# Self-attention's output product: seven tiles for four heads, with the first head's second tile moved by small transfers into idle rows of the other three's

## The chip, the cores and the metric

One core of one Trainium2 chip runs the whole kernel in one launch. The metric is the device time in microseconds, the median of several runs. TensorE multiplies matrices, ScalarE, VectorE and GpSimd (POOL in the rows) work on elements, and SyncE (SP in the rows) does nothing here but issue DMA transfers, one after another in the order in which they stand in its program.

## What is computed

A decoder layer over 32 sequences of 256 tokens with 256 features: self-attention, cross-attention against a context of 120 rows, and a mixture of 16 experts, each followed by a residual sum and a layer norm. The change lies in self-attention alone, 16 heads that share one latent of 72 columns:

```python
Wdkv = x @ latent_w + latent_b                                    # (b, t, 72), keys and values alike
q = einsum('btc,hcl->bhtl', x, Wd_w) + Wd_b                       # 16 heads of 72
scores = einsum('bhtl,bsl->bhts', q, Wdkv) / sqrt(16), causal
y = einsum('bhts,bsl->bhtl', softmax(scores), Wdkv)               # (b, h, t, 72)
z = transpose(y, (0, 2, 1, 3)).reshape(b, t, 16 * 72)
x = layernorm(x + z @ out_w + out_b)                              # the output product
```

## The kernel before

All products are of float32 values split in two: a high part, rounded to the format that TensorE takes at its fast rate, and a low part, what the rounding left. A product a x w is a_hi w_hi + a_lo w_hi + a_hi w_lo. For the general case that is three matmuls (`three`, L128 to L132). Where the contraction is over 72 rows only, a tile of TensorE's 128 rows has room for more than one of the three, and two matmuls do (`two`, L135 to L139):

- The first tile has y_hi[0:72] in rows 0 to 71 and y_hi[16:72] once more in rows 72 to 127, against w_hi[0:72] and w_lo[16:72].
- The second tile has y_lo[0:72] in rows 0 to 71 and y_hi[0:16] in rows 96 to 111, against w_hi[0:72] and w_lo[0:16]. Rows 72 to 95 are idle, against weights of zero. Rows above 111 are not read.

REST = 16 and AT = 96 are the names of these places, L = 72 is a head's rows. The repeated rows of y_hi come for free, since the latent has its columns repeated. The 16 rows in the second tile are a copy by GpSimd (L575), and y_lo is what VectorE subtracts (L909).

**The stage.** Two sequences are a group, and 16 groups make the stage. A group has 16 slots, u = 0 to 15, and slot g of the stage is for one pair of heads p = g % 16 // 2 and one sequence i = g % 2 of its group c. Each engine runs through the slots in the same order, with a lag for each step, so that in slot m there stand beside one another: scores of g = m - 6 (SL), normalising of m - 7 (IL), transposes of the probabilities of m - 8 (TL), the product with the values and y_hi, y_lo of m - 10 (PL), and the output product of m - 12 (OL). Buffers for y, q, and the probabilities are rings of 4 (RING). In 9 of the 16 slots (Q_SLOT: 2, 3, 5, 6, 8, 9, 11, 12, 14) a tile of q for both sequences is made: six matmuls, ScalarE's high part (L790), VectorE's low part (L898).

**The q moves.** A tile of q is 128 rows, and heads of 72 rows don't align with it. So SyncE moves the rows of each head from q_tile to their place in q by transfers within on-chip memory: the rows (L503), those that stand there twice (L506) and the 16 of the second tile (L510), 5 to 8 transfers a tile, 63 in a group. They have 8 to 72 partitions. The moves of tile t stand in SyncE's program in the slot of tile t, behind a wait for its low part (qlo_done). The scores of pair p (slot 2p + 6) wait on TensorE for tiles p and p + 1 (q_in), and ScalarE's high part of tile t waits for the moves of tile t - 2.

SyncE also loads xT for the next group in slot 3 (L412), the residual rows in slots 13 and 14 (L523), and stores x1 in slots 2 and 5 (L526). From slot 40 of the stage on it carries a staging of the cross-attention's weights, 16 pieces at 6 slots from one another: a load (L486) and, 6 slots later, two stores (L491).

The program's order on each engine is written out by hand in the `slot` functions of `sync`, `gpsimd`, `tensor`, `scalar` and `vector`; nothing reorders it. The body of 32 slots is a loop, with the first and last bodies written out.

The output product of a slot before, 8 matmuls of 256 columns:

```python
for hh in range(2):
    w = slice((2 * p + hh) * C, (2 * p + hh + 1) * C)
    for t in range(TT):
        mm = two(pe, O[i][:, t * C:t * C + C], y_hi[:, r, hh, tk], y_lo[:, r, hh, tk], ow[:, 0, w], ow[:, 1, w], ...)
```

Of the kernel before, what the change touches and what calls it, by code (L numbers as in the profile page):

```python
# [177 lines left out]
SA_BODY = 32  # L178
SA_BODIES = B * NP // SA_BODY
# [90 lines left out]
def self_attention(nc, al, bank, ident, cross, d):  # L270
# [13 lines left out]
    minus_low = al.sb("minus_low", [P, 1])  # L284
# [58 lines left out]
    ydup_done = al.sem("ydup_done")  # L343
    q_mm, qhi_done, qlo_done = al.sem("q_mm"), al.sem("qhi_done"), al.sem("qlo_done")
# [32 lines left out]
    sthi_done, stlo_done = Later(owhi_done, NP), Later(ow_done, NP)  # L377
# [28 lines left out]
    def sync(sp):  # L406
# [67 lines left out]
        def slot(J, m):  # L474
# [55 lines left out]
    def gpsimd(pool):  # L530
# [11 lines left out]
                           pattern=[[0, 1]], channel_multiplier=1).then_inc(const, 1)  # L542
# [13 lines left out]
        def slot(J, m):  # L556
# [14 lines left out]
            if slot_exists(J, g):  # L571
# [3 lines left out]
                pool.tensor_scalar(y_lo[AT:AT + REST, r], f32(y_hi[0:REST, r]), 1.0, 1.0, ALU.mult, ALU.mult).then_inc(ydup_done, 1)  # L575
# [33 lines left out]
    def tensor(pe):  # L609
# [33 lines left out]
        def slot(J, m):  # L643
# [77 lines left out]
            if slot_exists(J, g):  # L721
# [3 lines left out]
                if first_body(J) and c == 0 and i == 0:  # L725
                    pe.wait_ge(ow_done, p + 1)
# [13 lines left out]
    def scalar(act):  # L740
# [30 lines left out]
        def slot(J, m):  # L771
# [21 lines left out]
            if slot_exists(J, g):  # L793
# [4 lines left out]
                need(act, o_mm, upto_slot(J, g - RING))  # L798
                act.activation(y_hi[:, r].rearrange("l h t -> l (h t)"), PV[:], ACT.Copy).then_inc(yhi_done, 1)  # L799
# [1553 lines left out]
```

## Time and profile before

| | |
|---|---|
| median of 3 runs | 3112.0 us (3110.74 to 3114.18) |
| the profiled execution, its own time | 3109.2 us |
| its span, first to last instruction | 3107.3 us |
| mean granted TensorE clock | 0.998 |
| TensorE busy, share of the span | 99% |
| TensorE weight loads | 93% |
| VectorE / ScalarE / GpSimd | 73% / 69% / 51% |
| self-attention on TensorE | 0 to 1175 us |
| output product, first tiles | 1024 matmuls, 278.1 us busy, 303 ns each |
| output product, second tiles | 1024 matmuls, 257.6 us busy, 282 ns each |

The time is that of the run, the span that of the instructions in it. Busy times of matmuls overlap, as one starts while the one before it still runs: what a matmul costs is the distance between two starts. In the rows, PE is TensorE, PEld its weight loads, DVE VectorE, ACT ScalarE, POOL GpSimd, and SPq SyncE's queue, whose entries show how long an issue occupied it and not how long the transfer took. `<-` before a name gives who ended an idle time.

### The profile page before, as it was taken

How to read it: one execution, taken by the hardware profiler on the slowest of the kernel's cores; microseconds unless marked ns; L12 is line 12 of the kernel's file. 1: busy time of each engine (PE TensorE's matmuls, PEld its weight loads, DVE VectorE, ACT ScalarE, POOL GpSimd, SP SyncE). 2: the span in 40 equal slices, each digit the busy share in tenths (PEclk: the TensorE clock that was granted, in tenths of full speed). 3: DMA queues.
4: the chain of work that ended last, by engine and by line, in shares of the span. 5: the costliest groups of instructions: out<-in, count | busy, mean ns of one | idle time of the engine just before them, and what ended most of it. 6: DMA issues, size and time to landing. Idle time of an engine off the chain costs nothing. (4 is left out here: it accounts for less than half of the span.)

```text
span 3107.3 us, 72903 instructions
## 1 busy us (share of the span) xinstructions
PE 3080.1 (99%) x22657; PEld 2894.1 (93%) x22657; DVE 2259.1 (73%) x6587; ACT 2146.8 (69%) x6949; POOL 1591.9 (51%) x2918
## 2 busy tenths in 40 slices
PE   9999999999999999999999999999999999999998
PEld 7999999999999998999999999999988888889998
DVE  7888888887777877778878777887865555444665
ACT  8888888888888887787887877887744444442222
POOL 5677677666676665333333333333456666652000
PEclk9999999999999999999999999999999999999999
DMA  5455555444444460211111211211255445433333
GB/s 166 125 148 159 150 151 153 138 121 125 123 113 114 126 212 30 65 45 49 62 45 49 62 49 45 63 48 48 102 133 113 101 102 115 115 54 89 125 125 101
DMA packets 202273, 315.29 MB, mean 101 GB/s; under 512 B 34752, under 2 KB 135744, under 8 KB 200928
## 3 DMA queue, kind: packets, MB, share of 16 engines
q1 hardware_dynamic: 177376, 277.82, 29.6%
q0 software_dynamic: 24576, 33.57, 6.3%
q8 instruction: 155, 2.54, 0.4%
q14 instruction: 166, 1.36, 0.1%
HBM read 125.20 MB, written 75.50 MB: 65 GB/s over the span
## 5 line engine op out<-in xcount | busy, mean ns | idle before, releaser
L1131 POOL TENSOR_SCALAR ca_prob<-ca_prob,ca_inverse 128x120 f32<-128x120 f32 x1024 | 354.7, 365 | 618.9 <-DVE ca_inverse L1433 616.9
L820 ACT ACTIVATE sa_prob<-sa_prob,sa_shift 128x128 f32<-128x128 f32 (+1 forms) x1024 | 453.7, 462 | 0.0
L1373 ACT ACTIVATE ca_prob<-bank,ca_shift 128x120 f32<-128x120 f32 x1024 | 354.9, 368 | 3.5 <-DVE ca_shift L1427 2.2
L875 DVE CUSTOM_DVE_ANT_0 sa_prob<-bank,sa_mask 128x128 f32<-128x128 f32 (+1 forms) x1024 | 304.3, 351 | 0.9 <-issue 0.2
L566 POOL TENSOR_SCALAR sa_prob<-sa_prob,sa_inverse 128x128 f32<-128x128 f32 x512 | 199.4, 389 | 199.0 <-DVE sa_inverse L887 190.2
L137 PE MATMUL bank<-sa_ow,sa_y_hi 128*128 128x256 f32 x1024 | 278.1, 303 | 0.0
L139 PE MATMUL bank<-sa_kvT_b,sa_q 112*128 112x128 f32 (+1 forms) x1024 | 260.6, 280 | 0.0
L916 DVE TENSOR_TENSOR sa_pT_lo<-bank,sa_pT_hi 128x384 fp32r<-128x384 f32 x512 | 257.9, 543 | 0.2 <-ACT sa_pT_hi L807 0.2
L139 PE MATMUL bank<-sa_ow,sa_y_lo 112*128 112x256 f32 x1024 | 257.6, 282 | 0.0
L137 PE MATMUL bank<-sa_kvT_a,sa_q 128*128 128x128 f32 (+1 forms) x1024 | 248.9, 279 | 1.0 <-DVE sa_shift L875 0.7
L568 POOL TENSOR_SCALAR sa_prob<-sa_prob,sa_inverse 128x256 f32<-128x256 f32 x512 | 245.2, 479 | 0.0
L1866 POOL DMA_INDIRECT mid_acc<-ex_out,ex_to_tokens x112 | 191.1, 1706 | 87.4 <-DVE ex_out L2178 59.6
L909 DVE TENSOR_TENSOR sa_y_lo<-bank,sa_y_hi 96x512 fp32r<-96x512 f32 x256 | 174.9, 683 | 73.7 <-ACT sa_y_hi L799 73.2
L2056 ACT ACTIVATE ex_act_g<-bank 128x512 f32<-128x512 f32 x128 | 76.5, 598 | 215.2 <-PE bank L132 207.3
L807 ACT ACTIVATE sa_pT_hi<-bank 128x384 fp32r<-128x384 f32 x512 | 222.8, 493 | 0.5 <-PE bank L710 0.3
L1373 ACT ACTIVATION_READ_ACCUMULATOR ca_prob<-bank,ca_shift 128x1 f32 x1024 | 219.9, 215 | 0.0
L799 ACT ACTIVATE sa_y_hi<-bank 128x512 fp32r<-128x512 f32 x256 | 153.1, 598 | 95.6 <-PE bank L132 95.0
L820 ACT ACTIVATION_READ_ACCUMULATOR sa_prob<-sa_prob,sa_shift 128x1 f32 x1024 | 211.1, 206 | 0.0
L710 PE MATMUL bank<-all_ident,sa_prob 128*128 128x128 f32 x1536 | 209.8, 272 | 1.3 <-POOL sa_prob L568 1.3
L1333 ACT ACTIVATE ca_q_hi<-bank 128x256 fp32r<-128x256 f32 x256 | 99.0, 387 | 159.6 <-PE bank L132 153.4
L2143 DVE TENSOR_TENSOR ex_hid<-ex_act_g,bank 128x512 f32<-128x512 f32 x128 | 87.9, 687 | 162.2 <-PE bank L132 154.6
L137 PEld LDWEIGHTS bank<-sa_kvT_a,sa_q 128*128 128x128 f32 x1024 | 195.3, 191 | 2.1 <-DVE sa_shift L875 1.2
(274 smaller groups left out, 12039.2 us busy)
## 6 DMA issues: line engine op xcount, KB each, us to landing
sa_q<-sa_q_tile SPq DMA_DIRECT2D x125, 288.0 KB
sa_q<-sa_q_tile SPq DMA_DIRECT2D x157, 112.0 KB
mid_x2T<-ca_x2T SPq DMA_DIRECT2D x32, 512.0 KB, 3.0
ex_sx<-mid_x2T SPq DMA_DIRECT2D x32, 512.0 KB, 3.4
sa_q<-sa_q_tile SPq DMA_DIRECT2D x297, 32.0 KB
sa_xT_raw<-in_xT SPq DMA_DIRECT2D x32, 256.0 KB, 2.9
sa_q<-sa_q_tile SPq DMA_DIRECT2D x32, 256.0 KB
sa_x_res<-in_x SPq DMA_DIRECT2D x32, 256.0 KB, 3.0
```

The source lines that it names most:

```text
L137: pe.matmul(out, stat_hi, mov_hi, start=start, stop=False, skip_group_check=True)
L139: return pe.matmul(out, stat_lo[rows], mov_lo[rows], start=False, stop=stop, skip_group_check=True)
L566: pool.tensor_scalar(prob[:, r, hh, 0:P], prob[:, r, hh, 0:P], inverse[:, r, 2 * hh:2 * hh + 1], 1.0, ALU.mult, ALU.mult)
L568: pool.tensor_scalar(prob[:, r, hh, P:3 * P], prob[:, r, hh, P:3 * P], inverse[:, r, 2 * hh + 1:2 * hh + 2], 1.0, ALU.mult, ALU.mult).then ...
L710: mm = pe.transpose(TR[hh][:, n * P:n * P + P], prob[:, r, hh, n * P:n * P + P], ident[:])
L807: act.activation(pT_hi[:, r, hh], TR[hh][:, 0:3 * P], ACT.Copy).then_inc(pThi_done, 1)
L820: act.activation(prob[:, r, hh, cols], prob[:, r, hh, cols], ACT.Exp, bias=shift[:, r, n:n + 1], scale=-1.0, accum_out=total[:, r, n:n + 1 ...
L875: dve.tensor_tensor_reduce(out=prob[:, r, hh, cols], in0=SC[hh][:, t * T:t * T + (t + 1) * P], in1=mask[:].rearrange("p a s -> p (a s)")[: ...
L916: dve.tensor_tensor(pT_lo[:, r, hh], TR[hh][:, 0:3 * P], f32(pT_hi[:, r, hh]), ALU.subtract).then_inc(pTlo_done, 1)
L1131: ins = pool.tensor_scalar(prob[:, r, t, hh], prob[:, r, t, hh], inverse[:, r, n:n + 1], 1.0, ALU.mult, ALU.mult)
L1373: act.activation(prob[:, r, t, hh], SC[g % 2][:, n * S:n * S + S], ACT.Exp, bias=shift[:, r, n:n + 1], accum_out=total[:, r, n:n + 1]).the ...
L1866: pool.indirect_dma_start(d["acc"].rearrange("b t c -> (b t) c"), bass.IndirectOffsetOnAxis(ap=of[:, j:j + 1], axis=0), out[:, i, t], None ...
```

## The change

For a quad of four heads, two pairs, the first head loses its second tile. What stood in it is put into idle rows of the second tiles of the other three: y_lo[0:24] into rows 72 to 95 of head 1's, y_lo[24:48] into those of head 2's, y_lo[48:72] into those of head 3's, and y_hi[0:16] into rows 112 to 127 of head 2's. The weights' second tile (`ow_b`) is laid out on the host to match. Since partitions change, the rows go by DMA, four transfers on SyncE's queue in every slot of an even pair:

- the near one (L504 of the changed kernel), 24 partitions x 1 KB, in the slot in which y_lo is made, ahead of the q moves, behind a wait for ylo_done. It goes to the same pair's other head, and the output product of that pair waits for it (y_near) two slots later;
- the far ones (L529 to L531), 24, 16 and 24 partitions x 1 KB, after the q moves of that slot, behind a wait for the output product of two slots before in the ring (o_mm). They go to the next pair, whose output product waits for them (y_far) four slots later. ScalarE waits for them too, before it overwrites y_hi.

GpSimd's copy leaves out the first head, VectorE's y_lo has 72 partitions in place of 96, and the split of the output weights is two instructions in place of one, with a scalar of its own for each tile. In the output product all first tiles now come ahead of the second tiles.

```diff
+QUAD = 4
+GAP = AT - L
...
-    minus_low = al.sb("minus_low", [P, 1])
+    minus_low = al.sb("minus_low", [P, 2])
...
+            g = m - PL
+            if slot_exists(J, g) and g % QUAD < 2:
+                r, i = g % RING, g % 2
+                need_alone(sp, ylo_done, upto_slot(J, g), spare_sp)
+                sp.dma_start(f32(y_lo[L:AT, r, 1]), f32(y_lo[0:GAP, r, 0])).then_inc(y_near[i], 16)
             c, u = m // GROUP, m % GROUP
             t = tile_at(J, m)
...
+            g = m - PL
+            if slot_exists(J, g) and g % QUAD < 2:
+                r, i = g % RING, g % 2
+                n = (g + 2) % RING
+                need(sp, o_mm, upto_slot(J, g - 2))
+                sp.dma_start(f32(y_lo[L:AT, n, 0]), f32(y_lo[GAP:2 * GAP, r, 0])).then_inc(y_far[i], 16)
+                sp.dma_start(f32(y_lo[P - REST:P, n, 0]), f32(y_hi[0:REST, r, 0])).then_inc(y_far[i], 16)
+                sp.dma_start(f32(y_lo[L:AT, n, 1]), f32(y_lo[2 * GAP:L, r, 0])).then_inc(y_far[i], 16)
...
-                pool.tensor_scalar(y_lo[AT:AT + REST, r], f32(y_hi[0:REST, r]), 1.0, 1.0, ALU.mult, ALU.mult).then_inc(ydup_done, 1)
+                own = slice(int(g % QUAD < 2), 2)
+                pool.tensor_scalar(y_lo[AT:AT + REST, r, own], f32(y_hi[0:REST, r, own]), 1.0, 1.0, ALU.mult, ALU.mult).then_inc(ydup_done, 1)
...
-                for hh in range(2):
+                ahead = (y_near if p % 2 == 0 else y_far)[i]
+                for a, hh in ((0, 0), (0, 1), (1, 1)) if p % 2 == 0 else ((0, 0), (0, 1), (1, 0), (1, 1)):
                     w = slice((2 * p + hh) * C, (2 * p + hh + 1) * C)
+                    if a == 1 and hh == 1 - p % 2:
+                        need(pe, ahead, upto_quad(J, g, 16 if p % 2 == 0 else 48))
+                    rows = slice(0, AT + REST if a == 1 and (p % 2 == 0 or hh == 1) else P)
                     for t in range(TT):
                         tk = slice(t * P, t * P + P)
-
-                        mm = two(pe, O[i][:, t * C:t * C + C], y_hi[:, r, hh, tk], y_lo[:, r, hh, tk], ow[:, 0, w],
-                                 ow[:, 1, w], p == 0 and hh == 0 and t == 0, p == NP - 1 and hh == 1)
+                        mm = pe.matmul(O[i][:, t * C:t * C + C], (y_lo if a else y_hi)[rows, r, hh, tk], ow[rows, a, w],
...
+                if g % QUAD < 2:
+                    need(act, y_far[g % 2], upto_quad(J, g - QUAD, 48))
                 act.activation(y_hi[:, r].rearrange("l h t -> l (h t)"), PV[:], ACT.Copy).then_inc(yhi_done, 1)
...
-                dve.tensor_tensor(y_lo[0:AT, r].rearrange("l h t -> l (h t)"), PV[0:AT, :],
-                                  f32(y_hi[0:AT, r].rearrange("l h t -> l (h t)")), ALU.subtract).then_inc(ylo_done, 1)
+                dve.tensor_tensor(y_lo[0:L, r].rearrange("l h t -> l (h t)"), PV[0:L, :],
+                                  f32(y_hi[0:L, r].rearrange("l h t -> l (h t)")), ALU.subtract).then_inc(ylo_done, 1)
```

**SyncE, slots 2 and 3 of a group, before.** From the last moves of tile 0 (slot 2) to tile 1's last and the first load of xT. The shape is partitions x float32 elements of each.

```order
L506 DMA sa_q<-sa_q_tile 40x512
L510 DMA sa_q<-sa_q_tile 16x512
L526 DMA mid_x<-sa_x 128x2x256 [waits sa_x1_done]
L503 DMA sa_q<-sa_q_tile 16x1024 [waits sa_qlo_done,sa_s_mm]
L506 DMA sa_q<-sa_q_tile 16x512
L503 DMA sa_q<-sa_q_tile 72x1024
L506 DMA sa_q<-sa_q_tile 56x512
L510 DMA sa_q<-sa_q_tile 16x512
L503 DMA sa_q<-sa_q_tile 40x1024
L506 DMA sa_q<-sa_q_tile 24x512
L510 DMA sa_q<-sa_q_tile 16x512
L412 DMA sa_xT_raw<-in_xT 128x2x256 [waits sa_xlo_done]
```

**SyncE, the same place, changed** (the moves are now L516, L519 and L523, the store L547). From the same last moves of tile 0.

```order
L519 DMA sa_q<-sa_q_tile 40x512
L523 DMA sa_q<-sa_q_tile 16x512
L529 DMA sa_y_lo<-sa_y_lo 24x256 [waits early_sa_o_mm]
L530 DMA sa_y_lo<-sa_y_hi 16x256
L531 DMA sa_y_lo<-sa_y_lo 24x256
L547 DMA mid_x<-sa_x 128x2x256 [waits sa_x1_done]
L504 DMA sa_y_lo<-sa_y_lo 24x256 [waits sa_ylo_done]
L516 DMA sa_q<-sa_q_tile 16x1024 [waits sa_qlo_done,sa_s_mm]
L519 DMA sa_q<-sa_q_tile 16x512
L516 DMA sa_q<-sa_q_tile 72x1024
L519 DMA sa_q<-sa_q_tile 56x512
L523 DMA sa_q<-sa_q_tile 16x512
```

Three far transfers stand between tile 0's moves and the store, and a near one ahead of tile 1's moves. Tile 0's moves have a near one ahead of them in the same way, and three far ones follow tile 1's moves.

**TensorE, the output product of a slot and the scores of the next, before.**

```order
L137 MATMUL bank<-sa_ow,sa_y_hi 128x256 [waits sa_ydup_done,sa_ylo_done]
L139 MATMUL bank<-sa_ow,sa_y_lo 128x256
L137 MATMUL bank<-sa_ow,sa_y_hi 128x256
L139 MATMUL bank<-sa_ow,sa_y_lo 128x256
L137 MATMUL bank<-sa_ow,sa_y_hi 128x256
L139 MATMUL bank<-sa_ow,sa_y_lo 128x256
L137 MATMUL bank<-sa_ow,sa_y_hi 128x256
L139 MATMUL bank<-sa_ow,sa_y_lo 128x256
```

**TensorE, the same in a slot of an even pair, changed.**

```order
L759 MATMUL bank<-sa_ow,sa_y_hi 128x256 [waits sa_ydup_done,sa_ylo_done]
L759 MATMUL bank<-sa_ow,sa_y_hi 128x256 x3
L759 MATMUL bank<-sa_ow,sa_y_lo 128x256 [waits sa_y_near1]
L759 MATMUL bank<-sa_ow,sa_y_lo 128x256
L137 MATMUL bank<-sa_kvT_a,sa_q 128x128 [waits sa_s_read,sa_q_in1,sa_q_in0]
```

Six matmuls in place of eight, and a wait for the near transfer ahead of the last two. In a slot of an odd pair there are eight still, with a wait for the far ones ahead of the last four.

## Rows read from the trace of the kernel before

**Rows 1.** Windows: us, busy of each engine (instructions), PEclk, DMA share, GB/s.

```profile
100.00:200.00 100.00, 100.00 (x710) 93.22 (x709) 79.71 (x298) 82.03 (x268) 67.98 (x129) 1.00 0.50 135
700.00:800.00 100.00, 100.00 (x714) 93.29 (x713) 79.66 (x302) 80.89 (x263) 69.50 (x131) 1.00 0.41 115
...
1100.00:1200.00 100.00, 95.51 (x695) 89.80 (x694) 73.78 (x254) 72.93 (x253) 65.06 (x130) 0.98 0.46 154
```

**Rows 2.** Waits from 50 to 1170 us: total us, times, longest.

```profile
PEld bank L130 <- DVE sa_kv_lo L920: 2.3, 14, 0.2
...
PE bank L130 <- DVE sa_y_lo L909: 1.1, 2, 0.5
```

**Rows 3.** TensorE's timeline: starts of slots 0, 2, 6, 16, and two output matmuls.

```profile
706.38 0.22 PE L137 MATMUL bank<-sa_kvT_a,sa_q 128*128 128x128 f32 x1
...
715.40 0.22 PE L137 MATMUL bank<-sa_kvT_a,sa_q 128*128 128x128 f32 x1
...
719.88 0.28 PE L137 MATMUL bank<-sa_ow,sa_y_hi 128*128 128x256 f32 x1
...
720.36 0.28 PE L137 MATMUL bank<-sa_ow,sa_y_hi 128*128 128x256 f32 x1
...
734.17 0.22 PE L137 MATMUL bank<-sa_kvT_a,sa_q 128*128 128x128 f32 x1
...
778.46 0.22 PE L137 MATMUL bank<-sa_kvT_a,sa_q 128*128 128x128 f32 x1
```

**Rows 4.** The tile sa_q, SyncE, 706.4 to 778.4 us: ns min/median/max.

```profile
L503 SPq DMA_DIRECT2D sa_q<-sa_q_tile x24: 527/740/895, 719.7 to 775.6; - x24
L506 SPq DMA_DIRECT2D sa_q<-sa_q_tile x22: 583/748/807, 720.5 to 776.4; - x22
L510 SPq DMA_DIRECT2D sa_q<-sa_q_tile x17: 554/555/1788, 721.4 to 777.2; - x17
```

**Rows 5.** SyncE's timeline: partitions 128; 72; 16; 24; 16; 128; 24; 8.

```profile
705.76 0.58 SPq L523 DMA_DIRECT2D sa_x_res<-in_x  x1
719.70 0.79 SPq L503 DMA_DIRECT2D sa_q<-sa_q_tile  x1
...
724.99 0.55 SPq L503 DMA_DIRECT2D sa_q<-sa_q_tile  x1
...
729.29 0.72 SPq L506 DMA_DIRECT2D sa_q<-sa_q_tile  x1
730.05 0.56 SPq L510 DMA_DIRECT2D sa_q<-sa_q_tile  x1
730.65 1.09 SPq L412 DMA_DIRECT2D sa_xT_raw<-in_xT  x2
...
736.87 0.74 SPq L503 DMA_DIRECT2D sa_q<-sa_q_tile  x1
737.65 0.64 SPq L506 DMA_DIRECT2D sa_q<-sa_q_tile  x1
```

**Rows 6.** VectorE's timeline: y_lo of slot 2.

```profile
719.82 0.69 DVE L909 TENSOR_TENSOR sa_y_lo<-bank,sa_y_hi 96x512 fp32r<-96x512 f32 x1 [0.21 <-ACT sa_y_hi L799]
```

**Rows 7.** Timeline of the first group: a tile's last move, and who waited for it.

```profile
48.62 0.59 SPq L510 DMA_DIRECT2D sa_q<-sa_q_tile  x1
...
52.12 0.69 ACT L790 ACTIVATE sa_q_tile<-bank,sa_qbias 128x512 fp32r<-128x512 f32 x1 [2.24 <-DMA sa_q<-sa_q_tile]
```

**Rows 8.** DMA issues: KB each, median us from issue to landing.

```profile
mid_x<-sa_x SPq DMA_DIRECT2D x32, 256.0 KB, 2.3
```

**Rows 9.** SyncE's timeline: two pieces of the staging.

```profile
180.94 0.58 SPq L486 DMA_DIRECT2D early_st_raw<-in_wv  x1
...
182.05 0.85 SPq L491 DMA_DIRECT2D mid_cw<-early_st_lo  x1
...
452.40 0.39 SPq L486 DMA_DIRECT2D early_st_raw<-in_wq  x1
...
453.32 0.42 SPq L491 DMA_DIRECT2D mid_cw<-early_st_lo  x1
```

More of the change, by code:

```diff
@@ L202, in upto_tile, with upto_quad @@
     return J * (SA_GROUPS * QT * per) + (per * (t + 1) + more)
+def upto_quad(J, g, per=1):
+    return J * (SA_BODY // QUAD * per) + per * (g // QUAD + 1)
 def slot_exists(J, g):
@@ L343, in self_attention @@
     ydup_done = al.sem("ydup_done")
+    y_near, y_far = [al.sem(f"y_near{i}") for i in range(2)], [al.sem(f"y_far{i}") for i in range(2)]
     q_mm, qhi_done, qlo_done = al.sem("q_mm"), al.sem("qhi_done"), al.sem("qlo_done")
@@ L725, in slot @@
                 if first_body(J) and c == 0 and i == 0:
-                    pe.wait_ge(ow_done, p + 1)
+                    pe.wait_ge(ow_done, 2 * (p + 1))
                 if p == 0:
                     need(pe, o_read, upto_row(J, c, i - 2))
-                for hh in range(2):
+                ahead = (y_near if p % 2 == 0 else y_far)[i]
+                for a, hh in ((0, 0), (0, 1), (1, 1)) if p % 2 == 0 else ((0, 0), (0, 1), (1, 0), (1, 1)):
                     w = slice((2 * p + hh) * C, (2 * p + hh + 1) * C)
+                    if a == 1 and hh == 1 - p % 2:
+                        need(pe, ahead, upto_quad(J, g, 16 if p % 2 == 0 else 48))
+                    rows = slice(0, AT + REST if a == 1 and (p % 2 == 0 or hh == 1) else P)
                     for t in range(TT):
                         tk = slice(t * P, t * P + P)
-                        mm = two(pe, O[i][:, t * C:t * C + C], y_hi[:, r, hh, tk], y_lo[:, r, hh, tk], ow[:, 0, w],
-                                 ow[:, 1, w], p == 0 and hh == 0 and t == 0, p == NP - 1 and hh == 1)
+                        mm = pe.matmul(O[i][:, t * C:t * C + C], (y_lo if a else y_hi)[rows, r, hh, tk], ow[rows, a, w],
+                                       start=p == 0 and a == 0 and hh == 0 and t == 0, stop=p == NP - 1 and a == 1 and hh == 1,
+                                       skip_group_check=True)
                 mm.then_inc(o_mm, 1)
@@ L848, in split_ow @@
             dve.wait_ge(owhi_done, p + 1)
-            dve.scalar_tensor_tensor(out=part, in0=f32(part), scalar=minus_low[:, 0:1], in1=raw,
-                                     op0=ALU.mult, op1=ALU.add).then_inc(ow_done, 1)
+            for a in range(2):
+                cols = slice(C if a == 1 and p % 2 == 0 else 0, 2 * C)
+                dve.scalar_tensor_tensor(out=part[:, a, cols], in0=f32(part[:, a, cols]), scalar=minus_low[:, a:a + 1], in1=raw[:, a, cols],
+                                         op0=ALU.mult, op1=ALU.add).then_inc(ow_done, 1)
         def split_first_x(i):
@@ L2324, with filled @@
     ow = a("L0_attn_out_w").reshape(H, L, C).transpose(1, 0, 2).reshape(L, H * C)
+    def filled(h):
+        own, lent, n = ow[:, h * C:(h + 1) * C], ow[:, (h - h % QUAD) * C:(h - h % QUAD + 1) * C], h % QUAD
+        rows = np.zeros((P, C), ow.dtype)
+        if n > 0:
+            rows[:L], rows[L:AT], rows[AT:AT + REST] = own, lent[(n - 1) * GAP:n * GAP], own[:REST]
+        if n == 2:
+            rows[AT + REST:] = lent[:REST]
+        return rows
     laid = {
@@ L2331 @@
         "ow_a": again(ow, 0),
-        "ow_b": np.concatenate((ow, np.zeros((AT - L, H * C), ow.dtype), ow[:REST], np.zeros((P - AT - REST, H * C), ow.dtype))),
+        "ow_b": np.concatenate([filled(h) for h in range(H)], 1),
         "qbias": a("L0_attn_Wd_b").reshape(QT, P).T, "lbias": again(a("L0_attn_latent_b").reshape(L, 1), 0),
```

6 lines of the change are left out of this document (3 added, 3 removed).

## The prediction

> **What bounds the kernel now.** I read the windows by stage first, because the change lies in self-attention alone, the first 1175 us or so. In a window of that stage TensorE is busy for all of it, its weight loads for 93%, and VectorE, ScalarE and GpSimd for 70 to 81%, at the full granted clock [rows 1]. Next the list of waits of the stage: the longest of TensorE's that stand there total a few microseconds in 1120 [rows 2]. So a matmul that goes shortens the stage by its pitch, as long as nothing else takes over as the limit.
>
> The list of waits tells nothing of SyncE's queue, which is where the change adds its work. So I then read the queue's own timeline over one group of 16 slots, 706.38 to 778.46 us on TensorE, 72.1 us [rows 3]. In it SyncE issues 63 q moves [rows 4], 2 residual loads, 2 stores of x1 and 2 loads of xT. Each occupies it for 0.53 us or more, and they follow one another with gaps of about 0.04 us [rows 5]. By medians that is 24 x 0.74 + 22 x 0.75 + 17 x 0.555 = 43.7 us for the moves, 6 x 0.58 = 3.5 for the rest, 69 x 0.04 = 2.8 of gaps: **SyncE is occupied for 50.0 of 72.1 us**. The largest idle piece, 13.4 us, lies in slots 15, 0 and 1 of the group, which have few moves or none (706.34 to 719.70) [rows 5].
>
> **What the change takes away.** TensorE: the second tile of one head in four, 2 matmuls in each of 128 slots, 256 in all. The pitch is 0.12 us (719.88 to 720.36 is four of them, start to start) [rows 3]. 16 go in a group, 1.92 us, and 256 x 0.12 = **30.7 us** in all. That the others now run as all the first tiles and then all the second ones I cost at nothing: the two kinds have the same pitch. GpSimd copies half as much in half the slots, VectorE writes 72 partitions in place of 96 over the same 512 columns: neither is the limit, nothing in the sum. The split of the output weights becomes 16 instructions in place of 8, off TensorE's path: nothing.
>
> **What it adds.** Four transfers in every second slot, 32 in a group, 512 in all, of which 24 of the 32 move 24 partitions and 8 move 16. The size of such a transfer has no row, but its number of partitions has: the q moves of 24 partitions occupied SyncE for 0.72 and 0.74 us, those of 16 for 0.55 and 0.56, one of 8 for 0.64 [rows 5]. The cost does not go by bytes (72 partitions of 4 KB took 0.79, 24 of 2 KB 0.72). I take 0.74 and 0.56; the bounds are 0.53 (the lowest of all moves [rows 4]) and 0.79 (72 partitions [rows 5]). That gives 24 x (0.74 + 0.04) + 8 x (0.56 + 0.04) = 23.5 us, and SyncE's load becomes 50.0 + 23.5 = **73.5 us in a group that TensorE would do in 72.1 - 1.9 = 70.2**. The queue does not fit any more.
>
> The Trainium skill (DMA: Bandwidth & Descriptors, "Why a DMA increments its semaphore by 16 and not by 1") says that a transfer is spread over the largest number of DMA engines up to 16 that divides its rows, which would put 24 rows on 12 engines and 16 rows on 16. The trace's issue times part along the same line. Were bytes to set the cost instead, the 24-row transfers would be priced as the 16-row ones, and the time would be that of the second case below.
>
> Two waits on SyncE add to this, since its queue is served in order. *The first:* the near transfer waits until VectorE has written y_lo, and the q moves of the same slot stand behind it. *The second:* the far transfers wait for an output product, and stand before the next slot's moves. Where does TensorE feel it?
>
> *Slot 6.* The scores of slot 6 want tile 1 of q, moved in slot 3. y_lo of slot 2 is done at 719.82 + 0.69 = 720.5 [rows 6], less 4 x 0.12 gained in slots 0 and 1, 720.0. Then the near transfer 0.78; tile 0's moves and the store 5.3 (719.70 to 724.99); three far transfers 2.2; a near one 0.78; tile 1's moves 5.7 (724.99 to 730.65) [rows 5]: 734.8. The landing comes on top. It has no row of its own for q moves. A store of 256 KB takes 2.3 us from its issue [rows 8], 1.7 from the end of its issue; once, at 52.12 us, ScalarE waited for a tile's moves whose last issue ended at 49.21, 2.9 us before [rows 7]. With 1.7 to 2.9 (I take 2.0) tile 1 is there at 736.8; TensorE, 8 x 0.12 earlier than the 734.17 of before [rows 3], wants it at 733.2: a wait of 3.6 us in each group, against 1.9 gained.
>
> *The turn of the group.* SyncE, once behind, has no more idle time from slot 2 to slot 15. The output product of slot 1 needs the near transfer issued in slot 15. So the group's period closes over a loop: SyncE's load without the last three far transfers, 73.5 - 2.2; the landing, 2.0; the last two matmuls of slot 1, 0.2; slot 2 of TensorE up to its y_lo, which the next near transfer waits for, 715.40 to 720.51, 5.1 [rows 3, 6]. That is 78.6 us in place of 72.1, **6.5 us more in a group** (slot 6's wait is a part of it and not to be added). The first group has output products in four of its 16 slots only; I count the other 15 groups: 97.5 us.
>
> *The staging.* 16 pieces of the cross weights pass through this queue in the groups after the second: a load and two stores each, 1.3 us (452.40 to 453.74) to 2.0 us (180.94 to 182.90) [rows 9]. Before, idle time took them in; now they lengthen the loop, save for the 3 slots in 16 in which SyncE still idles: 16 x 1.6 x 13/16 = 21 us.
>
> The end of the stage already has 4.5 us in which TensorE idles (95.51 of 100 [rows 1]); a late queue could add up to 5, left to the range.
>
> **The sum.** The profiled execution took 3109.2 us around its span of 3107.3. 3109.2 + 97.5 + 21 = 3227.7; the 30.7 us gained are in the 6.5 us a group already, as the loop does not go over TensorE's saved matmuls. The median of the runs before is 3112.0, 0.1% above the profiled one. I forecast **3228 us, 3.7% slower**. Such a loop is a calculation from one group; its terms move it as follows. Landing 2.9: +14. 24-row issues at 0.79: +18. At 0.66: -29.
>
> **The rivals.**
>
> *A. The queue takes the transfers in.* The issue cost of a small transfer would be well under that of any row. The slot 6 chain says where it turns: 720.0 + 5.3 + 5.7 + 1.7 = 732.7 plus five added issues must be under 733.2, so no wait at all needs 0.1 us each; the wait stays below the 1.9 us gained up to (0.5 + 1.9) / 5 = 0.5 us each. At 0.1 the whole gain comes, 3109.2 - 30.7 = 3078.5 us; at 0.5, none. For it: DMA share 0.41 to 0.50 [rows 1], so the DMA engines have room. Against: the lowest of all 63 moves is 0.527 us [rows 4]. Faster gets 0.04, no change (within 0.2%, about what a measurement of this kernel can tell) 0.03. The Trainium skill speaks for this rival (DMA: Bandwidth & Descriptors, "Issuing engines are not separate DMA queues"): the time a sequencer takes to initiate a DMA "is usually small relative to the DMA itself". By that the time would be 3078.5; the trace shows a queue occupied 0.55 to 0.8 us for each.
>
> *B. The loop closes less tightly.* The 24-row transfers cost like the 16-row ones (0.56 + 0.04). SyncE's load is 50.0 + 32 x 0.6 = 69.2, under TensorE's 70.2; the loop gives 69.2 - 1.8 + 7.3 = 74.7, 2.6 a group, 39 us, and the staging in part, 15: 3163 us. For it: 1 KB rows, half the size of the smallest moves. Against: the 8-partition move of 0.64. Chance 0.2, range 3125 to 3195.
>
> *C. As forecast, 3195 to 3270:* 0.73.
>
> **How the numbers follow.** C is the likeliest, so 3228. Slower: C and B, 0.93; same 0.03; faster 0.04. The range for 8 in 10 leaves out the lower part of B and the tail above landing and issue both at their upper bounds: 3150 to 3264.
>
> **What would show it.** In the changed kernel's trace: SyncE issues of y_lo from 24 partitions at 0.7 us or more, near 0.56 from 16; no idle time of SyncE over 1 us from slot 2 to slot 15; groups of about 78 us; TensorE idle before the first score matmul of slot 6 by 3 to 4 us until a q move lands, and before a y_lo matmul of slot 1 by 2 to 3 us until a near transfer does; some 1100 us of stage become some 1290; TensorE's busy share of the stage falls from 100 to about 90%. Cross-attention and the rest unchanged. It would be wrong if issues of 0.3 us stood there, if SyncE did idle in mid-group, or if TensorE had no wait in slot 6.

## The result and the profile after

| | before | changed |
|---|---|---|
| median | 3111.7 us | 3282.1 us (3275.0 to 3285.7, 4 runs) |
| ratio | | 1.0546, 95% interval 1.0533 to 1.0558 |
| the profiled execution | 3109.2 us | 3280.1 us |
| mean granted TensorE clock | 0.998 | 0.977 |
| TensorE busy, weight loads | 99%, 93% | 95%, 89% |
| last output product of self-attention starts | 1174.8 us | 1344.5 us |

5.5% slower, where 3.7% was forecast. It lies above the range (3150 to 3264) by 18 us. The whole loss is in self-attention: from its last output product to the end of the span there are 1932.5 us before and 1933 us now.

The windows of the changed kernel (columns as in [rows 1]); the stage now lasts past 1300 us:

```profile
100.00:200.00 100.00, 93.47 (x647) 86.17 (x646) 73.91 (x280) 77.28 (x251) 61.81 (x120) 0.98 0.46 121
700.00:800.00 100.00, 92.50 (x643) 85.55 (x643) 73.60 (x278) 75.43 (x248) 61.80 (x123) 0.98 0.44 118
1200.00:1300.00 100.00, 91.28 (x619) 83.48 (x619) 71.62 (x276) 71.65 (x241) 55.76 (x115) 0.97 0.42 113
```

No engine is full any longer, where TensorE was 100% [rows 1]. Its list of waits from 50 to 1350 us, against the one of [rows 2], with totals of 1 and 2 us, and behind it SyncE's own:

```profile
PE bank L759 <- DMA sa_y_lo<-sa_y_lo: 66.7, 29, 5.8
PE bank L137 <- DMA sa_q<-sa_q_tile: 49.0, 15, 4.3
PE bank L130 <- DVE sa_y_lo L939: 12.5, 12, 2.9
...
SPq L77 <- DVE sa_y_lo L939: 87.1, 17, 7.9
SPq L516 <- PE bank L139: 27.9, 60, 0.8
SPq L460 <- PE bank L139: 8.1, 1, 8.1
```

L77 is the line of a helper that waits and then counts up a spare semaphore. TensorE waits for transfers for 116 us: 49 for q moves, once in each of 15 groups, which is slot 6; the rest for the y_lo transfers, 44.7 of it in 16 waits in slot 1. SyncE's one large wait is for y_lo of slot 2, once in a group (17 in all). The issues, from 300 to 1200 us (ns min/median/max), cost what the rows of the q moves said [rows 5]:

```profile
L531 SPq DMA_DIRECT2D sa_y_lo<-sa_y_lo x88: 728/729/1762, 299.3 to 1198.4; - x88
L504 SPq DMA_DIRECT2D sa_y_lo<-sa_y_lo x88: 716/747/1306, 308.4 to 1199.2; - x88
L529 SPq DMA_DIRECT2D sa_y_lo<-sa_y_lo x87: 719/738/1066, 313.1 to 1197.0; - x87
L530 SPq DMA_DIRECT2D sa_y_lo<-sa_y_hi x87: 512/554/1171, 313.9 to 1197.8; - x87
```

SyncE's timeline at the turn of a group, and on to the last move of tile 1 and the far transfers behind it:

```profile
319.92 0.42 SPq L499 DMA_DIRECT2D mid_cw<-early_st_lo  x1
326.66 0.75 SPq L504 DMA_DIRECT2D sa_y_lo<-sa_y_lo  x1
327.52 0.75 SPq L516 DMA_DIRECT2D sa_q<-sa_q_tile  x1
...
340.58 0.56 SPq L523 DMA_DIRECT2D sa_q<-sa_q_tile  x1
341.18 0.73 SPq L529 DMA_DIRECT2D sa_y_lo<-sa_y_lo  x1
```

It idles from 320.34 to 326.66, where 13.4 us were idle before, and then not again for over 1 us until the next turn: in 900 us (150 to 1050) it has 64 us of idle pieces over 0.3 us, against 244 us before. TensorE in the same group, and windows of it (us, busy of the five engines, PEclk as the last but two):

```profile
339.45 0.40 PE L759 MATMUL bank<-sa_ow,sa_y_lo 112*128 112x256 f32 x2
342.91 0.45 PE L137 MATMUL bank<-sa_kvT_a,sa_q 128*128 128x128 f32 x1 [3.06 <-DMA sa_q<-sa_q_tile]
...
345.19 0.63 PE L131 MATMUL bank<-sa_xT_lo,sa_wd_hi 128*128 128x512 f32 x1
345.61 0.63 PE L132 MATMUL bank<-sa_xT_hi,sa_wd_lo 128*128 128x512 f32 x1
```

```profile
343.00:348.00 5.00, 5.00 (x16) 4.32 (x17) 1.38 (x9) 0.44 (x1) 1.63 (x4) 0.50 0.63 189
349.00:355.00 6.00, 6.00 (x52) 5.87 (x51) 4.41 (x16) 5.71 (x20) 3.63 (x8) 1.00 0.56 146
```

Tile 1's last move ends its issue at 341.14 and TensorE starts at 342.91, 1.8 us later: slot 6's wait is there, 3.1 us, where 3.6 was forecast. Behind it the granted clock is 0.50, the 1.2 GHz level, and matmuls of 512 columns start 0.42 us apart. That was in no term of the sum.

**The balance of the miss.** A group's start is here its first matmul of the latent (about 1 us behind its first score). The groups start at 60.30 and 1213.17 us in the first and last of 15 places, 82.35 us apart on average, against 72.12 before. So 14 periods cost 143.2 us more, the last group with the drain behind it 24.2 (131.3 us from its start to its last output product, against 107.1), the beginning 2.3: 170 in all. The forecast had 118.5: 7.9 for each of 15 groups.

### The profile page after: what moved, and what is told of

It reads as the page before. It is cut to its first block and busy times, and to the rows that moved or that the text cites. A ratio compares the mean times of both kernels' runs of the same rounds, so it can differ in the third digit from the quotient of the medians.

```text
span 3277.6 us, 73039 instructions
## 1 busy us (share of the span) xinstructions
PE 3122.0 (95%) x22401; PEld 2913.9 (89%) x22401; DVE 2252.4 (69%) x6595; ACT 2139.5 (65%) x6949; POOL 1566.1 (48%) x2918
## 5 line engine op out<-in xcount | busy, mean ns | idle before, releaser
L137 PE MATMUL bank<-sa_kvT_a,sa_q 128*128 128x128 f32 (+1 forms) x1024 | 263.5, 292 | 49.8 <-DMA sa_q<-sa_q_tile 49.0
L139 PE MATMUL bank<-sa_kvT_b,sa_q 112*128 112x128 f32 (+1 forms) x1024 | 268.7, 287 | 0.0
L816 ACT ACTIVATE sa_q_tile<-bank,sa_qbias 128x512 fp32r<-128x512 f32 x141 | 96.9, 687 | 250.9 <-PE bank L132 192.3
L137 PEld LDWEIGHTS bank<-sa_kvT_a,sa_q 128*128 128x128 f32 x1024 | 204.1, 199 | 55.2 <-issue 52.5
L928 DVE SCALAR_TENSOR_TENSOR sa_q_tile<-bank,sa_qbias,sa_q_tile 128x512 fp32r<-128x512 f32 x141 | 105.4, 747 | 183.9 <-ACT sa_q_tile L816 183.9
L939 DVE TENSOR_TENSOR sa_y_lo<-bank,sa_y_hi 72x512 fp32r<-72x512 f32 x256 | 174.6, 682 | 81.8 <-ACT sa_y_hi L827 81.7
L139 PEld LDWEIGHTS bank<-sa_kvT_b,sa_q 112*128 112x128 f32 x1024 | 204.6, 200 | 0.0
```

The costliest lines, as they stand in the source:

```text
L137: pe.matmul(out, stat_hi, mov_hi, start=start, stop=False, skip_group_check=True)
L139: return pe.matmul(out, stat_lo[rows], mov_lo[rows], start=False, stop=stop, skip_group_check=True)
```

## The experiments

Times are medians, ratios are to the kernel before on the same chip (3109.2 to 3109.7 us), with the 95% interval. A period is the mean distance of group starts in the profiled execution. The load is the time in which SyncE issues, with the gaps under 0.3 us between issues; what is longer is its idle time.

**1. Seven tiles and no transfers.** The two blocks on SyncE, both waits for them and the narrower y_lo are undone.

```diff
-                sp.dma_start(f32(y_lo[L:AT, r, 1]), f32(y_lo[0:GAP, r, 0])).then_inc(y_near[i], 16)
...
-                need(sp, o_mm, upto_slot(J, g - 2))
-                sp.dma_start(f32(y_lo[L:AT, n, 0]), f32(y_lo[GAP:2 * GAP, r, 0])).then_inc(y_far[i], 16)
...
-                        need(pe, ahead, upto_quad(J, g, 16 if p % 2 == 0 else 48))
...
-                    need(act, y_far[g % 2], upto_quad(J, g - QUAD, 48))
```

> The seven tiles and their order stay, the 512 transfers and every wait for them are gone, so the moved rows' products are left out of the output (second tiles read 112 rows of their own). Theory (SyncE's queue is the whole loss): TensorE is the limit again, 256 matmuls of 0.12 us fewer than before, 3112 - 31 = 3081 us, no wait for q in slot 6. Rival 1 (the new order of the tiles, or the split of the weights, costs): more than 3090. Rival 2 (another engine is the limit once TensorE has less to do): between 3090 and 3112, with TensorE idle in the short slots.

Measured: 3081.8 us, 0.991 (0.989 to 0.993), as the theory had it; period 70.38, most groups 70.27. Its window:

```profile
700.00:800.00 100.00, 99.78 (x705) 92.68 (x704) 79.53 (x303) 81.62 (x266) 70.36 (x137) 1.00 0.47 130
```

TensorE gives back 28 of the 30.7 us; what else is left of the change costs under 3 us. So the loss, 200 us against this kernel, is the transfers' and their waits'.

**2. The same issues, awaited by nobody.** The transfers copy a constant into idle memory, from slot 20 of the stage on.

```diff
-                sp.dma_start(f32(y_lo[L:AT, r, 1]), f32(y_lo[0:GAP, r, 0])).then_inc(y_near[i], 16)
...
+                if not idle:
+                    sp.dma_start(behind[L:AT, i * C:i * C + C], mask[0:GAP, 0:2].rearrange("l a s -> l (a s)")).then_inc(y_near[i], 16)
```

> As seven_alone, but SyncE issues the same four transfers at the same places behind the same waits of its own; they carry constants into idle memory and neither TensorE nor ScalarE waits for them (the first 20 slots have none). The moved rows' products are left out. Theory (the queue's occupation): the wait for q in slot 6 stays at 3 to 4 us a group with the slow clock behind it, the wait for a y_lo row in slot 1 is gone; groups of 76 to 78 us, 3185 to 3215 us. Rival (the waits of TensorE for the transfers' landing are the loss, the queue itself has room): about 3081, like seven_alone.

Measured: 3217.6 us, 1.035 (1.033 to 1.037), clock 0.985. TensorE's waits:

```profile
PE bank L137 <- DMA sa_q<-sa_q_tile: 51.8, 14, 5.7
PE bank L130 <- DVE sa_y_lo L952: 24.8, 22, 3.3
PE bank L774 <- DMA sa_behind<-sa_mask: 13.1, 1, 13.1
```

The third is my kernel's own: the last slots wait for the copies. The period is 79.0 us once the transfers are there, and SyncE idles for 17 us in 900: its queue alone takes 8.7 of the 12 us that a group has lost against experiment 1. The price of occupying the queue is thus the larger part, the waits for what was moved the smaller. The split is good to about 1 us: SyncE's load is 77.5 us a group here, against 76.5 in the changed kernel. The theory's range was missed by 2.6 us; its rival, 3081, by 137.

**3. 16 partitions in place of 24.** Eight rows of each of the 24-partition transfers are left where they are, after the first two slots.

```diff
-                sp.dma_start(f32(y_lo[L:AT, r, 1]), f32(y_lo[0:GAP, r, 0])).then_inc(y_near[i], 16)
+                e = GAP if first_body(J) and g < 2 else REST
+                sp.dma_start(f32(y_lo[L:L + e, r, 1]), f32(y_lo[0:e, r, 0])).then_inc(y_near[i], 16)
```

> The changed kernel with the 24-partition transfers cut to 16 partitions (8 rows of each are left out, but for the first quad). Theory (what an issue costs goes by whether the partitions are a multiple of 16, 0.56 against 0.75 us): the three issues drop to 0.55 to 0.60 us, SyncE's load by 24 x 0.17 = 4 us a group, the time to 3170 to 3210. Rival (the cost goes by bytes or is fixed): issues stay at 0.7 us or above, the time within 15 us of the changed kernel's 3282.

Measured: 3245.0 us, 1.044 (1.042 to 1.046), period 79.96. The issues from 300 to 1200 us:

```profile
L505 SPq DMA_DIRECT2D sa_y_lo<-sa_y_lo x91: 507/518/1314, 301.8 to 1194.2; - x91
L531 SPq DMA_DIRECT2D sa_y_lo<-sa_y_lo x91: 535/587/1567, 306.3 to 1199.3; - x91
L532 SPq DMA_DIRECT2D sa_y_lo<-sa_y_hi x90: 528/589/1657, 306.9 to 1187.7; - x90
L533 SPq DMA_DIRECT2D sa_y_lo<-sa_y_lo x90: 580/589/1773, 307.5 to 1188.3; - x90
```

0.52 to 0.59 in place of 0.73 to 0.75: the price of an issue goes down from 24 partitions to 16. This run takes a third of the bytes away too; that bytes alone don't set the price is shown by the q moves, where 16 partitions of 2 KB (32 KB) took 0.56, less than 24 of 1 KB here. The price doesn't simply rise with the partitions either: 128 took 0.58 and 8 took 0.64 [rows 5]. 37 us is all it brought: the expectation of 3170 to 3210 was missed by 35, and the prediction's case B, this very kernel, was worked out as 3163. That sum was 82 us too low, and only in small part for the price.

**4. The clock held up.** Matmuls into a bank that nothing reads fill TensorE's waits in slots 6 and 1.

```diff
+            if m % GROUP == 6 and group_exists(J, m // GROUP) and not (first_body(J) and m < GROUP):
+                need(pe, qlo_done, upto_tile(J, m // GROUP * QT + 2))
+                fill(Q[:], 11)
...
+                        if m % GROUP == 1:
+                            need(pe, ylo_done, upto_slot(J, m - PL))
+                            fill(PV[:], 8)
```

> The changed kernel with matmuls that nobody reads where TensorE would wait: 11 of 512 columns ahead of the scores of slot 6 and 8 ahead of the near wait of slot 1, in every group but the first; 2.6 and 1.9 us at full clock. Theory (the 52 us by which the forecast was short are mostly the half clock after each idle stretch, which lengthens slot 2 inside the loop): the granted clock stays near 1.0 and the time falls to 3220 to 3250. Rival (the clock's loss is hidden behind SyncE's queue): the clock rises, the time stays within 10 us of 3282. If the fillers overshoot the waits: above 3282.

Measured: 3269.0 us, 1.051 (1.050 to 1.053). The window that had 0.50:

```profile
343.00:348.00 5.00, 4.09 (x27) 3.73 (x27) 2.04 (x10) 1.13 (x2) 1.64 (x4) 1.00 0.50 157
```

The clock is back there (0.98 on average from 50 to 1350 us, against 0.94), the time is not: 13 us of 170, in neither range of the expectation and nearer to the rival's. The fillers in slot 6 did not overshoot: in all 15 groups TensorE still waited for the q moves behind them, 12.5 us in all. The clock falls as a result of the waits and most of what it costs is time in which TensorE would have waited for SyncE anyway.

**5. The near transfer behind the q moves.**

```diff
-                sp.dma_start(f32(y_lo[L:AT, r, 1]), f32(y_lo[0:GAP, r, 0])).then_inc(y_near[i], 16)
             c, u = m // GROUP, m % GROUP
...
+                sp.dma_start(f32(y_lo[L:AT, r, 1]), f32(y_lo[0:GAP, r, 0])).then_inc(y_near[i], 16)
...
                 need(sp, o_mm, upto_slot(J, g - 2))
```

> The changed kernel with the near transfer issued behind the q moves of its slot in place of ahead of them; nothing else. Theory (a loop through SyncE's full queue sets the period, of which slot 6's wait is a part that costs nothing more): the wait in slot 6 shrinks from 3 to 4 us to some 2, since tile 0's and tile 1's moves no longer stand behind y_lo and a near transfer, but the queue's load stays; only the 0.9 us from q's low part to y_lo leaves the turn of the group, 3282 - 15 x 0.9 = 3268, within 3255 to 3280. Rival (slot 6's wait and the slow clock behind it are a loss of their own): 3282 - 15 x (1.8 + 1.5) = 3232.

Measured: 3278.4 us, 1.055 (1.054 to 1.057), within the theory's 3255 to 3280.

```profile
PE bank L759 <- DMA sa_y_lo<-sa_y_lo: 123.1, 57, 7.1
...
PE bank L137 <- DMA sa_q<-sa_q_tile: 3.0, 2, 2.0
```

Slot 6's 49 us are gone and the waits for y_lo have taken 56 more. The two together are 126 us in place of 116, and the time is the same within 4 us. Where the load is well above TensorE's, the order inside the queue decides who waits, and hardly how long the kernel takes.

**6. Fewer issues.** The far transfers of both sequences go together, 20 issues in a group in place of 32, near ones behind the q moves (6a) or ahead of them as in the changed kernel (6b).

```diff
+            if slot_exists(J, g) and g % QUAD == 2:
+                need(sp, ylo_done, upto_slot(J, g - 1))
+                need(sp, o_mm, upto_slot(J, g - 3))
+                sp.dma_start(f32(y_lo[L:AT, 2:4, 0]), f32(y_lo[GAP:2 * GAP, 0:2, 0])).then_inc(y_far[0], 16)
+                sp.dma_start(f32(y_lo[P - REST:P, 2:4, 0]), f32(y_hi[0:REST, 0:2, 0])).then_inc(y_far[0], 16)
+                sp.dma_start(f32(y_lo[L:AT, 2:4, 1]), f32(y_lo[2 * GAP:L, 0:2, 0])).then_inc(y_far[0], 16)
```

> The same rows moved, with 20 issues a group in place of 32: the three far transfers serve both sequences at once, issued in slots 0, 4, 8 and 12 of the group, and the near ones stand behind the q moves. Theory: load 50 + 8 x 0.80 + 8 x 0.80 + 4 x 0.62 = 65.3 us in a group of 70.2, so the queue idles again and the loop opens; slot 6's wait 0 to 1 us, 3085 to 3115 us. Rival (the transfers harm by something else than the number of issues, such as the landing time of a near one): above 3160.

> As far_merged (three far transfers for both sequences together), but the near transfer ahead of the q moves of its slot, as in the changed kernel, in place of behind them. Nothing is left out. far_merged took 3188.9 us with groups of 77.4; in its group at 700 us TensorE waited 2.8 us for a near transfer issued behind seven moves, two in a row. SyncE's load is some 70 us a group with or without, as TensorE's. Theory: the late near transfer alone held far_merged; then groups fall to 71 to 74 us and the time to 3095 to 3140. Rival: at a load equal to TensorE's any order only moves the wait to another place (here to the q moves, and so to the scores): time within 20 us of 3189, TensorE's waits now at the scores for q moves, over 20 us in the stage.

Measured: 6a 3188.9 us, 1.025 (1.024 to 1.027), period 77.4; 6b 3167.9 us, 1.019 (1.018 to 1.021), period 75.1. 6a missed its 3085 to 3115 by far, and the theory that only the late near transfer held it missed in 6b as well (3095 to 3140). Its rival, within 20 us of 3189 with over 20 us of waits at the scores, missed the time by 1 us and had the waits:

```profile
PE bank L758 <- DMA sa_y_lo<-sa_y_lo: 26.5, 21, 7.3
PE bank L137 <- DMA sa_q<-sa_q_tile: 23.7, 15, 2.2
```

SyncE's load is now 70 us a group (69.8 to 70.3), as much as TensorE's, and a merged 24-partition transfer occupies it for 0.85 and 0.79 us, not 0.74. What I had left out is the idle at the turn: a queue that is full from slot 2 on, and idles for 5 us once in a group behind y_lo, closes at 75 even when its load equals TensorE's 70.3. In 6a the idle time is 7.4 us a group. That 6b is faster than 6a by 21 us shows that at equal loads the order does count for something.

**7. The same transfers on ScalarE's queue.**

```diff
+            g = m - 1 - PL
+            if slot_exists(J, g) and g % QUAD < 2:
...
+                need(act, ylo_done, upto_slot(J, g))
+                act.dma_start(f32(y_lo[L:AT, r, 1]), f32(y_lo[0:GAP, r, 0])).then_inc(y_near[i], 16)
+                need(act, o_mm, upto_slot(J, g - 2))
+                act.dma_start(f32(y_lo[L:AT, n, 0]), f32(y_lo[GAP:2 * GAP, r, 0])).then_inc(y_far[i], 16)
...
```

> The changed kernel with all four transfers issued by ScalarE, one slot later, ahead of its y_hi, where what they wait for is done. SyncE then has its load of before. Theory A (an issue occupies the engine that gives it as long as it does SyncE, 0.56 to 0.75 us): ScalarE is busy for 58 us of a group already, 23.5 more make 82: as slow as the changed kernel or slower, 3260 to 3330. Theory B (the issue costs ScalarE's own stream under 0.1 us each): 3085 to 3100.

Measured: 3182.7 us, 1.023 (1.022 to 1.025), between the two theories' ranges; period 76.7. ScalarE's timeline:

```profile
708.53 0.73 ACTq L810 DMA_DIRECT2D sa_y_lo<-sa_y_lo  x1
708.71 0.21 ACT L845 ACTIVATION_READ_ACCUMULATOR sa_prob<-sa_prob,sa_shift 128x1 f32 x1
708.80 0.52 ACT L845 ACTIVATE sa_prob<-sa_prob,sa_shift 128x256 f32<-128x256 f32 x1
...
709.30 0.80 ACTq L812 DMA_DIRECT2D sa_y_lo<-sa_y_lo  x1
...
710.84 0.75 ACTq L814 DMA_DIRECT2D sa_y_lo<-sa_y_lo  x1
711.71 0.60 ACT L824 ACTIVATE sa_y_hi<-bank 128x512 fp32r<-128x512 f32 x1 [1.44 <-PE bank L132]
```

An issue takes ScalarE's sequencer as long as SyncE's. Activations already handed over run beside it, so it is not simply added (theory A), but the next y_hi is late, and TensorE waits 74.8 us in 83 times for the y_lo made from it. So this place also costs, at half the price: 101 us over experiment 1, where SyncE's queue costs 200.

**8. The end of the stage.** SyncE's loads for cross-attention stand behind the transfers of their slot, the output weights two slots later.

```diff
-    WV_IN, WK_IN, WQ_HI_IN, WQ_LO_IN, WO_IN = 0, 1, 2, 4, 6
+    WV_IN, WK_IN, WQ_HI_IN, WQ_LO_IN, WO_IN = 0, 1, 2, 4, 8
...
-            if isinstance(J, int) and J == SA_BODIES:
-                load_weights(m)
...
+            if isinstance(J, int) and J == SA_BODIES:
+                load_weights(m)
...
         return slot
```

> The changed kernel, but in the stage's last slots SyncE's loads for the cross-attention (its weights, first x and context) stand behind the near and far transfers of their slot in place of ahead of them, and the last of them (the output weights, which wait for the stage's last scores) two slots later. Nothing is left out. In the changed kernel's trace SyncE stood 8.1 us behind that wait, and the last near transfers came late: TensorE waited 3.8 us at 1305.7 and 5.8 us at 1324.9. Theory: the last group's loss, larger than forecast, comes in part from these loads being in front of the transfers. Then the last two waits shrink by 4 to 9 us and the time is 3282 - 4 to 9 = 3273 to 3278, the waits for near transfers after 1300 us under 5 us in all. Rival: the last transfers are late because of the queue's backlog and of y_lo itself, the loads are innocent: time within 3 us of the changed kernel's 3282, the two waits as they were.

Measured: 3284.3 us (3276.8 to 3290.1), 1.056 (1.054 to 1.058): nothing that the time shows. TensorE's late waits, of the changed kernel and then of this one:

```profile
1305.70 0.80 PE L759 MATMUL bank<-sa_ow,sa_y_lo 112*128 112x256 f32 x2 [3.79 <-DMA sa_y_lo<-sa_y_lo]
1324.91 0.80 PE L759 MATMUL bank<-sa_ow,sa_y_lo 112*128 112x256 f32 x2 [5.80 <-DMA sa_y_lo<-sa_y_lo]
```

```profile
1311.56 0.79 PE L759 MATMUL bank<-sa_ow,sa_y_lo 112*128 112x256 f32 x2 [4.32 <-DMA sa_y_lo<-sa_y_lo]
1327.87 0.80 PE L759 MATMUL bank<-sa_ow,sa_y_lo 112*128 112x256 f32 x2 [2.80 <-DMA sa_y_lo<-sa_y_lo]
```

The last group with its drain is 3 us shorter (128.3 in place of 131.3), while the periods before it were 0.4 us longer in this execution. The two waits shrank by 2.5 us together, less than the theory's 4 to 9. By these two executions the loads' share is 3 us, less than the 13 us by which the executions of one kernel differ; SyncE's 8.1 us behind them were mostly time it had.

**9. The rows made in place.** PV's rows 72 to 127 hold columns 16 to 71 once more, so VectorE can write y_lo[16:72] of the first head straight into rows 72 to 127 of the second head's tile. The instruction starts at row 64; rows 64 to 71 are written over by the subtraction behind it. Only y_lo[0:16] and the first 16 rows of both y_hi are left to move, two transfers of 16 partitions for both sequences: 8 issues in a group in place of 32.

```diff
+            if slot_exists(J, g) and g % QUAD == 2:
...
+                need(sp, o_mm, upto_slot(J, g - 3))
+                sp.dma_start(f32(y_lo[L:L + REST, 2:4, 0]), f32(y_lo[0:REST, 0:2, 0])).then_inc(y_far[0], 16)
+                sp.dma_start(f32(y_lo[P - REST:P, 2:4]), f32(y_hi[0:REST, 0:2])).then_inc(y_far[0], 16)
...
+                if g % QUAD < 2:
+                    dve.tensor_tensor(y_lo[64:P, r, 1], PV[64:P, 0:T], f32(y_hi[64:P, r, 0]), ALU.subtract).then_inc(y_ext, 1)
```

> Seven tiles in another layout: 56 of the first head's 72 low rows come into rows 72 to 127 of the second head's second tile by one more VectorE subtraction of 64 partitions x 256 columns out of the columns that stand there twice, without a transfer; the last 16 rows and the 16-row copies of the first two heads go by two 16-partition transfers for both sequences at once, 8 issues a group in place of 32. Theory: SyncE's load 50 + 8 x 0.62 = 55 us in 70.2, no wait of TensorE for a transfer, 3081 to 3087 us, and faster than both kernels. Rival (VectorE, 80% busy, becomes the limit by 3 us more in a group, as y_lo comes later for the next product): 3090 to 3112, with TensorE idle before the products with the values.

The two repairs, of which the second is the edit of experiment 8:

```diff
-                need(sp, ylo_done, upto_slot(J, g + 1 if first_body(J) and g == 2 else g - 1))
+                need(sp, ylo_done, upto_slot(J, g - 1))
...
+                if first_body(J) and g == 0:
+                    dve.memset(f32(y_lo[64:AT, 2:4]), 0.0).then_inc(y_ext, 1)
```

> As engine_rows (16-row pieces and two transfers per quad of heads, the rest of the rows made by VectorE in place), with two edits: the idle rows of the first two target buffers are cleared once ahead of the first y_lo, so that the first two transfers need not wait for slot 3's y_lo; and the loads for cross-attention stand behind the transfers in the last slots, as in end_freed. Nothing is left out. engine_rows took 3098.9 us with steady groups of 70.2, its first group starting 8.3 us later than that of seven_alone (65.1 against 56.9), behind a SyncE wait of 7.8 us for y_lo, two groups of 71.4 and 72.0, and some 9 us lost from the last group on. Theory: the first 8 us are that wait, and 1 to 3 us of the end are the loads; time 3087 to 3092, first group's start 57 to 59 us. Rival: what is lost at the start is VectorE's added instruction and the slower fill, which these edits leave: 3096 to 3101.

Measured: 3098.9 us, 0.9965 (0.995 to 0.998), and with the two repairs 3088.6 us, 0.993 (0.992 to 0.995): **faster than both kernels, by 0.7% and 5.9%**. The first missed its 3081 to 3087 by 12 us; it lies in the rival's range, but its steady groups of 70.2 us show that VectorE is not the limit. The second lies in its 3087 to 3092. Of the second:

```profile
L500 SPq DMA_DIRECT2D sa_y_lo<-sa_y_lo x39: 636/675/703, 311.0 to 977.9; - x39
L501 SPq DMA_DIRECT2D sa_y_lo<-sa_y_hi x39: 565/590/1114, 311.7 to 978.6; - x39
```

```profile
700.00:800.00 100.00, 99.59 (x707) 92.47 (x706) 85.16 (x319) 82.54 (x272) 67.66 (x127) 1.00 0.46 124
```

Steady groups take 70.2 us, as in experiment 1; VectorE pays with 85 us of 100 in place of 80. The first repair moved the first group's start from 65.1 to 60.2 us (57 to 59 expected), so about 3 of the 8 us are not that wait; the rival puts them to the fill and VectorE's added work, which no run separates. What separates it from experiment 1 is 7 us by the medians, 10.6 in the profiled executions: 3.3 at that start, 2.0 in the groups (one took 72.5), 2.5 in the last group and 2.8 behind the stage.

## Why the prediction was right in direction and too low

*Right, by its own steps.* TensorE's gain (experiment 1: 28 of 30.7). The bound that changes: SyncE's queue. The price of an issue by its partitions, 0.74 and 0.56: measured 0.73 to 0.75 and 0.55, and experiment 3 shows that it goes with 24 against 16. Slot 6's wait, 3.6 forecast, 3.1 in the group shown and 49.0 / 15 = 3.3 on average. The near transfer's wait at the turn, 2 to 3 forecast, 44.7 / 16 = 2.8. No idle time of SyncE in mid-group. Rival A fell on the issue price: 32 issues of 24 KB or less took 22.4 us of SyncE's time in a group of 82. The Trainium skill (DMA: Bandwidth & Descriptors, "Issuing engines are not separate DMA queues") calls the time to initiate a DMA "usually small relative to the DMA itself". For these transfers the trace disagrees: 0.73 to 0.75 us of issue, where TensorE went on 1.8 us after the issue of a q move had ended.

*The step that failed is the loop's sum:* three of its terms were too small, the gaps between issues, the way from slot 2 to y_lo, and the length at which the last group was counted. It came to 78.6 a group, with the staging 80.0, against 82.35. In terms of 150 to 1050 us of the trace, per group:

| | forecast | measured |
|---|---|---|
| SyncE's load without its waits, staging in it | 73.5 + 1.4 = 74.9 | (772.8 + 63.7) / 900 x 82.35 = 76.5 |
| what the turn adds | 5.1 + 2.0 + 0.2 - 2.2 = 5.1 | 64.0 / 900 x 82.35 = 5.9 |
| period | 80.0 | 82.4 |

- *The gaps*, 1.7 a group. I took 0.04 between issues, from rows of q moves that follow one another [rows 5]. From 150 to 1050 us the changed kernel has 0.12 ahead of the near transfers and ahead of the first move of a tile, and 0.045 ahead of the other moves and transfers. The wait is not what costs it: the first far transfer (L529) waits too and has 0.044 ahead of it. The trace has one more instruction between the issues in the dearer places, a semaphore instruction of the helper at L77. Before, it was 0.13 in the 20 places where a tile's first move stands behind a store of x1, so the trace of the kernel before had this price. The gaps sum to 5.8 us, not 4.1. The rest nearly balances, by luck: staging 1.9 and not 1.4, q moves 43.1 and not 43.7, transfers 22.4 and not 22.2, the loads and stores of x 3.2 and not 3.5.
- *The turn*, 0.8. The way from slot 2 to its y_lo was taken from a trace at full clock. SyncE's idle there is mostly 4.8 to 7.9 us. Two of the long ones, 6.3 at 320 and 7.9 us at 404, have a granted clock of 0.64 and 0.55 in the windows 320 to 327 and 404 to 411: TensorE had just come out of its own wait for the near transfer. Of the 11 idle pieces at a turn the 6 behind a stretch of half clock are 6.4 us long on average, the other 5 are 4.3. Experiment 4, which holds the clock up, has 56.7 / 900 x 82.0 = 5.2 us there, as forecast. (In its profiled execution the load was 0.3 a group higher, so that its period is only 0.4 shorter: what of its 13 us comes from the turn is not shown.)
- *The last group*, 16.3. I counted it as one of 15; from its start to its last output product the last one is 107.1 / 72.09 = 1.5 groups long, since the output product lags by six slots behind the scores. At 10.2 us a group 15 of its 24 us are that, an estimate, and the cross-attention's loads are about 3 (experiment 8). The remaining 6 were not separated; half clock behind the wait at 1305.7 lies in them (0.55 from 1306 to 1312).

Together: 14 x 2.33 = 32.6 (a period grew by 10.23 and not by 7.9), the end 24.2 - 7.9 = 16.3, the beginning 2.3: the 51.2 us between 118.5 and 169.7.

*Case B was mis-worked as well.* Experiment 3 is that case: its load is 73.4 us a group, where I had 69.2, and its idle time 6.5 against 5.5. In the 4.2 are 2.0 of staging, 1.8 of gaps and 0.8 of issues at 0.54 to 0.62 on average, not 0.56, less 0.3 of the rest. With the turn added, a load only just under TensorE's 70.2 does not let the queue catch up (experiment 6b: load 70, period 75); the staging, which I counted in part, then counts in full. The same oversight stands in my expectation for 6a, which added no idle at the turn at all.

*Where the gain went:* experiment 2 puts 8.7 of the 12 us a group to the queue's time alone, the turn and the waits for the moved rows make the other 3.3. The waits of experiment 5 move but don't shrink. Of the last group's 24 us, 6 remain without a cause.

## What to carry to other kernels

Before work moves to a queue that has slack on average, sum its occupied time over one period and count every issue at the price of its like, and 0.08 us more where another instruction of the queue's engine stands between two issues; then look for the place in the period where it must wait for the engine it feeds, and add that idle time to the load before you compare it with the period (a load of 70 us and 5 of idle time gave 75 here, where TensorE needs 70.3; a load of 58, in experiment 9, cost nothing). A drain is part of a period too: count the last group by its length. If rows are needed on other partitions, look first whether an engine that already writes them can write them there (here the repeated columns did), and move only the rest, in few and wide transfers.

## What the hardware showed that was not expected

- After an idle time of 3.1 us of TensorE the granted clock was 0.50 from 342.9 until nearly 349 us, with the matmuls' pitch twice as long (0.42 for 512 columns). With the wait filled by unread matmuls it stayed at 1.00. Not every such wait was followed by a fall: behind one of 3.0 us that ended at 490.2 the clock was 1.00 from 487 to 495.
- An issue on ScalarE's queue took 0.74 for 24 partitions and 0.57 for 16, as on SyncE's, but with activations running beside it.
- A transfer of 24 partitions x 2 rows of 1 KB took SyncE 0.85 and 0.79 us (medians of 47 each in experiment 6a), one of 1 row 0.74; one of 16 partitions x 2 rows of 1 KB 0.68, one of 1 row 0.55. Merging two transfers saves 0.5 to 0.7 us, not the whole second one.
